# A two-layer language tower on one core: sums in the output tensor, norm weights in the products, halved second-tile products, identity products between two passes

## The chip, the cores and the metric

The kernel runs on one core of a Trainium2 chip. The metric is the device time of one execution in microseconds (us). The core has a matmul engine (TensorE, PE in the rows; PEld is its weight load), a vector engine (VectorE, DVE), an activation engine (ScalarE, ACT), a general engine (GpSimd, POOL) and an engine that only issues transfers (SyncE, SP). Each runs its own instruction stream in order; they meet at semaphores. Matmuls write into eight PSUM banks; DVE and ACT read them; POOL cannot.

## What is computed

A batch of 32 sequences of 128 tokens, 192 features each, goes through an embedding and four blocks, each with a residual sum. Cut to what matters here:

```
h = layernorm(emb[x] * sqrt(192) + positions)
h = h + quantised_attention(layernorm(h))       # 12 heads of 16; softmax(scores) is rounded to 8 bits with one
                                                # scale for the whole tensor, so it needs two passes over the scores
h = h + three_expert_attention(layernorm(h))
h = h + latent_block(layernorm(h)):
    lat = silu(rmsnorm(x, ln_w) @ w_comp);  q, k, v = lat @ w_qkv
    out = linear attention of elu(q)+1, elu(k)+1, gated v, with a decay per head    # scores * decay, then times v
    x = x + (rmsnorm(out, memn_w) @ w_proj) * silu(lat @ w_outgate)
    x + (silu(rmsnorm(x, ffn_ln_w) @ w1) * (rmsnorm(x, ffn_ln_w) @ w2)) @ w3
h = h + attention(...) and then a mixture of 8 experts, 2 per token:
    out = x + sum over its 2 experts of weight * (gelu(xm @ w1[e] + b1[e]) @ w2[e] + b2[e])
```

`rmsnorm(x, w)` multiplies the normed features by a vector `w` before the product, so `w` may as well stand in the rows of the weight matrix.

## The kernel before

The stages run one after the other. The embedding and the quantised attention work on eight groups of four 128-token tiles. **The second pass of the quantised attention** (`tensor_attn`, from the function `turn_terms` on) follows the first when all row sums are known: DVE forms the largest reciprocal of a sum, PE turns it across the partitions in `tensor_tops(pe, SUM_TOP, 0, 1)` (L315, L317), DVE makes three bf16 terms of each row's exponent offset (L463 to L467), PE turns these (L625, `turn_terms`), ACT takes them (L726), and then, for each of 32 tiles, PE forms scores in four banks (L640, L641: products of 32 rows), ACT takes exponentials of 128x384 (L735), DVE adds a shift (L481), and PE multiplies by the values (L650, L654).

**The latent block** works on 16 pairs of tiles. Two streams, each with its own four banks and buffers, take turns: while one runs the first part of a pair (`tensor_l_1`, `scalar_l_1`, `vector_l_1`, `pool_l_1`), the other runs the second part (`..._l_2`), and `alternate` writes their pieces into each engine's one stream in turn at every `yield`. Of the first part matter here: normed rows are turned (`turn`, L966), ACT takes them out of PSUM multiplied by `l_lnw` (`take_turned`, L977, one instruction for each half of the features), PE forms the latent (L1007) and from it q, k, v and the gates (L1718, L1721). Later `products` (L1662) makes 12 score matrices of a tile: for each of three `k`, four products of 32 rows, one for each bank `j`. `decayed` (L1577) multiplies each bank of 384 columns by the decay and writes it to SBUF. This is done for tile 0 and then for tile 1 in the same four banks: the second `products` waits until DVE has read all four banks, and the second `decayed` waits until all 12 products are there. Between the two `products` stands half of the other stream's last product (L1759), and behind the second the other half. Then `times_v` (L1672) multiplies both tiles by the values, waiting first for all eight `decayed` steps; ACT takes the result (L1819), PE turns it back (L1680), DVE divides (L1586 to L1588), and PE turns it once more.

Of the second part matter: `turn_doubled` (L985, L987) turns the normed rows of the feed-forward, `take_doubled` (L993) takes them out of PSUM multiplied by `l_fnw`, again one ACT instruction for each half, and `hidden` (L1690 with 128 rows, L1698 with 64 rows) multiplies by w1 and w2. The tables of this block are made by `vector_l_tables` on DVE, behind the last but one piece of the three-expert stage; its last step folds `memn_w` into `w_proj` (L1425).

**The expert stage** sorts the tokens' rows by expert into a DRAM tensor, `moe_rows_in`, and takes 39 groups of 256 rows, the last of each expert filled up with unused rows of weight 0. Meanwhile the residual rows have been written to another DRAM tensor, `moe_sum` (in the code `acc`; L2020, a POOL transfer for each pair). For each group PE runs L2359, L2364, two turns (L2346, L2347) and L2374; DVE weights the results (L2262) into one of three buffers `x_y`; POOL issues two indirect transfers that add 128 rows each to `moe_sum` (L2291) and waits for them to land before the next group. Unused rows are sent to spare rows behind row 4095. DVE may refill a buffer when the adds of three groups earlier have landed. SP loads the next group's weights. At the end SP waits for all adds, copies `moe_sum` to the output (L2332) and waits for that copy.

The wait that splits the two tiles of the latent block, and the end of the program:

```
if i >= 1:
    pe.wait_ge(f.decayed, per(g, 4 * M, 4 * i))        # products, tile 1
v.wait_ge(f.qk_p, per(g, M, i + 1))                    # decayed
pe.wait_ge(f.decayed, per(g, 4 * M, 4 * M))            # times_v, both tiles
...
sp.wait_ge(x_add, 32 * NX)
sp.dma_start(flat(out...), flat(acc[0:T * P, :])).then_inc(x_end_st, 16)
sp.wait_ge(x_end_st, 16)
```

Of the kernel before, what the change touches and what calls it, by code (L numbers as in the profile page):

```python
# [6 lines left out]
F32 = mybir.dt.float32  # L7
# [88 lines left out]
def tower(nc, a, out):  # L96

    with ExitStack() as ctx:
# [437 lines left out]
        def tensor_attn(pe):  # L536
# [80 lines left out]
            tensor_tops(pe, SUM_TOP, 0, 1)  # L617

# [371 lines left out]
        def take_doubled(a, b, dst, ready, scale):  # L990

            for c in range(2):
                ins = nc.scalar.activation(dst[:, c, :], a.bank[b][:, c * NM:(c + 1) * NM], ACT.Identity, scale=scale[:, c:c + 1])  # L993
            ins.then_inc(ready, 1)
# [413 lines left out]
        def vector_l_tables(v, ch):  # L1408

            yield  # L1410
            v.wait_ge(s_wf, 16 * len(loads_f + loads_l))
            ch.step(nc.vector.tensor_scalar(l_qkn, l_qkn, ROOT_SCALE, None, ALU.mult))
            for s in range(2):
                w = l_qkn[:, s * DH:(s + 1) * DH]
                nc.vector.tensor_tensor(l_cw[:, s, :], l_rot[:, 0:DH], w, ALU.mult)
                nc.vector.tensor_tensor(l_sw[:, s, 0:8], l_rot[:, 16:24], w[:, 8:16], ALU.mult)
                nc.vector.tensor_tensor(l_sw[:, s, 8:16], l_rot[:, 24:32], w[:, 0:8], ALU.mult)
            v.wait_ge(l_s1, 1)
            ch.step(nc.vector.tensor_scalar(l_ld, l_ld, 1.0, None, ALU.add))
            ch.step(nc.vector.reciprocal(l_ld, l_ld))  # L1420
            ch.step(nc.vector.tensor_scalar(l_ld, l_ld, 0.65, 0.3, ALU.mult, ALU.add))
            ch.step(nc.vector.tensor_scalar(l_ld, l_ld, 1e-5, 0.999, ALU.max, ALU.min))
            nc.vector.tensor_scalar(l_dt, l_ld, -1.0, 1.0, ALU.mult, ALU.add).then_inc(l_s0, 1)
            for c in range(2):
                ins = nc.vector.tensor_scalar(lw_proj[0:C, c, :], lw_proj[0:C, c, :], l_memn[0:C, c:c + 1], None, ALU.mult)  # L1425
            ch.step(ins)
# [146 lines left out]
        def decayed(v, g, a, f, i):  # L1573

            v.wait_ge(f.qk_p, per(g, M, i + 1))
            for j in range(4):
                nc.vector.tensor_tensor(a.p[:, 4 * i + j, :], a.bank[j][:, 0:384], decay[:, j, :],  # L1577
# [75 lines left out]
        def products(pe, g, a, f, i):  # L1653
# [3 lines left out]
            if i >= 1:  # L1657
                pe.wait_ge(f.decayed, per(g, 4 * M, 4 * i))
            for k in range(3):
                for j in range(4):  # L1660
                    s = slice(32 * j, 32 * j + 32)
                    mm = nc.tensor.matmul(a.bank[j][:, k * P:(k + 1) * P], a.ts[s, i, 3 + k, :], a.ts[s, i, k, :],  # L1662
                                          start=True, stop=True)
            mm.then_inc(f.qk_p, 1)

        def times_v(pe, g, a, f, i):

            pe.wait_ge(f.value, per(g, 1, 1))
            pe.wait_ge(f.decayed, per(g, 4 * M, 4 * M))
# [112 lines left out]
        def scalar_l_1(act, g, a, f):  # L1782
            act.wait_ge(f.xT_p, per(g, 3, 1))
            take_turned(a, 0, a.xT, f.xT, scale=l_lnw)
# [43 lines left out]
        def scalar_l_2(act, g, a, f):  # L1828
# [4 lines left out]
            take_doubled(a, 2, a.xT, f.xT, l_fnw)  # L1833
# [176 lines left out]
        def send(pool, g, a, f):  # L2010
# [9 lines left out]
            pool.dma_start(acc[bass.ds(pair * (M * P), M * P), :].rearrange("(t p) d -> p t d", p=P),  # L2020
# [171 lines left out]
        acc = nc.dram_tensor("moe_sum", (T * P + NR, D), F32).ap()  # L2192
# [94 lines left out]
        def pool_x(pool):  # L2287
            for k in range(NX):
                pool.wait_ge(x_out, k + 2)
                for t in range(NT):  # L2290
                    pool.indirect_dma_start(out=acc, out_offset=bass.IndirectOffsetOnAxis(  # L2291
                        ap=x_id[k % B3][:, t:t + 1].bitcast(U32), axis=0), in_=x_y[k % B3][:, t, :], in_offset=None,
                        compute_op=ALU.add).then_inc(x_add, 16)
                pool.wait_ge(x_add, 32 * (k + 1))

        def sync_x(sp):
# [34 lines left out]
            flat = lambda x: x.rearrange("r d -> (r d)").rearrange("(p n) -> p n", p=P)  # L2331
            sp.dma_start(flat(out.rearrange("t p d -> (t p) d")), flat(acc[0:T * P, :])).then_inc(x_end_st, 16)  # L2332
            sp.wait_ge(x_end_st, 16)
# [223 lines left out]
```

## Time and profile before

| | |
|---|---|
| median of 3 runs | 1969.83 us (1968.5 to 1972.9) |
| profiled execution, its own time | 1969.73 us |
| its span, first to last instruction | 1968.1 us |
| mean granted clock of TensorE | 0.892 of full |
| busy share of the span: PE / DVE / ACT / POOL | 79% / 66% / 49% / 24% |
| second pass of the quantised attention | about 352 to 424 us |
| latent block | about 684 to 1178 us, a period of 56.9 us for two pairs |
| expert stage, groups | about 1610 to 1950 us |
| copy to the output | from 1955.8 us to the end |

```text
span 1968.1 us, 37567 instructions
## 1 busy us (share of the span) xinstructions
PE 1551.7 (79%) x13020; PEld 1205.5 (61%) x13020; DVE 1289.9 (66%) x4233; ACT 961.6 (49%) x2769; POOL 481.7 (24%) x689
## 2 busy tenths in 40 slices
PE   0076764888888758888888877999999949999996
PEld 0032221776666546666666656777777738888885
DVE  7898885787888767877877744666666642222221
ACT  1275999873545445554454423444444414444442
POOL 7401333000000012222222211222222223333332
PEclk9985555559999869999999988999999969999998
DMA  3000000119991000000000000000000038778785
GB/s 74 18 1 1 1 1 1 22 42 172 183 174 11 0 1 1 0 0 0 0 0 0 0 10 18 26 25 24 24 24 24 25 89 199 190 193 199 189 197 137
DMA packets 136263, 113.02 MB, mean 57 GB/s; under 512 B 29416, under 2 KB 128456, under 8 KB 136136
## 3 DMA queue, kind: packets, MB, share of 16 engines
q1 hardware_dynamic: 119320, 91.70, 20.3%
q0 software_dynamic: 16864, 20.33, 5.4%
q8 instruction: 42, 0.69, 0.1%
q14 instruction: 37, 0.30, 0.1%
HBM read 69.19 MB, written 45.94 MB: 59 GB/s over the span
## 4 chain that ended last, share of the span: by engine, by line
PE 46%; DVE 34%; ACT 12%; issue 4%; POOL 2%; DVEq 0%; DMA 0%; ACTq 0%; POOLq 0%; SPq 0%
ACT bank L716 9%; PE bank L2374 8%; PE bank L2364 6%; PE bank L1007 5%; PE bank L2359 3%; PE bank L1000 3%; PE bank L2030 2%; PE bank L1690 2%; DVE R L1577 2%; DVE WK L1577 2%; DVE R L1882 2%; PE bank L966 1%; PE bank L640 1%; PE bank L641 1%; PE bank L1718 1%
## 5 line engine op out<-in xcount | busy, mean ns | idle before, releaser
L1047 POOL TENSOR_TENSOR WK<-WK,mhalf 128x2 f32<-128x2 f32 (+1 forms) x96 | 78.7, 819 | 546.0 <-DVE WK L1024 247.1
L2411 ACT ACTIVATE R<-bank,R 128x256 f32<-128x256 f32 x234 | 98.5, 472 | 187.1 <-PE bank L2364 185.5
L716 ACT ACTIVATE bank<-bank,nbias,sc 128x128 f32<-128x128 f32 x384 | 168.9, 952 | 21.6 <-POOL nbias L528 21.6
L2291 POOL DMA_INDIRECT moe_sum<-WK x78 | 121.5, 1558 | 229.0 <-DMA moe_sum<-WK 166.2
L2262 DVE SCALAR_TENSOR_TENSOR WK<-bank,R,WK 128x192 f32<-128x192 f32 x78 | 28.9, 412 | 207.6 <-PE bank L2374 207.6
L716 ACT ACTIVATION_READ_ACCUMULATOR bank<-bank,nbias,sc 128x1 f32 x384 | 162.1, 726 | 0.0
L2374 PE MATMUL bank<-R 128*128 128x192 f32 x936 | 158.6, 326 | 0.0
L1007 PE MATMUL bank<-WK,R 96*128 96x256 f32 x576 | 147.5, 398 | 6.2 <-ACT WK L973 3.5
L2374 PEld LDWEIGHTS bank<-R 128*128 128x128 f32 x936 | 151.3, 190 | 0.1
L1007 PEld LDWEIGHTS bank<-WK,R 96*128 96x128 f32 x576 | 106.2, 194 | 25.9 <-ACT WK L973 6.6
L2364 PE MATMUL bank<-R 128*128 128x256 f32 x468 | 113.0, 392 | 0.0
L610 PE MATMUL bank<-R 32*128 32x128 bf16 x384 | 62.8, 300 | 60.1 <-ACT bank L716 57.2
L610 PEld LDWEIGHTS bank<-R 32*128 32x128 bf16 x384 | 29.5, 118 | 118.7 <-ACT bank L716 106.6
L2364 PEld LDWEIGHTS bank<-R 128*128 128x128 f32 x468 | 86.8, 192 | 23.8 <-issue 13.2
L433 DVE TENSOR_REDUCE neg_all<-bank 128x3 f32<-128x384 f32 x128 | 69.4, 554 | 27.4 <-PE bank L610 25.2
L528 POOL TENSOR_SCALAR nbias<-neg_all,sc 128x3 f32<-128x3 f32 x128 | 38.8, 303 | 197.6 <-DVE neg_all L433 197.3
L559 PE MATMUL bank<-R,wq 96*128 96x512 bf16 x192 | 79.4, 542 | 4.6 <-DVE WK L407 2.7
L1000 PE MATMUL bank<-R,WK 96*128 96x192 f32 x384 | 76.4, 343 | 2.9 <-ACT WK L973 1.4
L1690 PE MATMUL bank<-WK,R 128*128 128x256 f32 x256 | 65.5, 400 | 15.0 <-ACT WK L993 15.0
L315 PE MATMUL bank<-ident,amx 128*1 128x128 f32 (+2 forms) x5 | 1.9, 382 | 93.6 <-DVE amx L351 54.8
L2140 ACT ACTIVATE WK<-bank,R 128x256 f32<-128x256 f32 x96 | 40.3, 471 | 69.4 <-PE bank L1007 69.4
L966 PE MATMUL bank<-ident,WK 128*96 128x128 f32 x320 | 53.0, 290 | 26.1 <-DVE WK L1899 11.6
(507 smaller groups left out, 4131.3 us busy)
## 6 DMA issues: line engine op xcount, KB each, us to landing
moe_rows_in<-zeros SPq DMA_DIRECT2D x1, 25026.0 KB, 147.2
R<-in_L_ffn_w SPq DMA_DIRECT2D x39, 576.0 KB, 5.0
R<-in_L_ffn_w SPq DMA_DIRECT2D x39, 384.0 KB, 3.1
R<-moe_rows_in SPq DMA_DIRECT2D x39, 194.0 KB, 4.6
R<-in_L_ffn_w SPq DMA_DIRECT2D x78, 96.0 KB, 3.7
R<-in_L_ffn_b SPq DMA_DIRECT2D x39, 96.0 KB, 5.1
moe_sum<-resid POOLq DMA_DIRECT2D x16, 192.0 KB
moe_sum<-WK POOLq DMA_INDIRECT x78, 5.9
```

The lines of the kernel that those rows point to most:

```text
L559: mm = nc.tensor.matmul(bank[b][:, :], wq[0:C, c, o * P:(o + 1) * P], tokens(xqT_all, g)[0:C, c, :], start=(c == 0), stop=(c == 1))
L610: mm = nc.tensor.matmul(bank[u % 4][:, k * P:(k + 1) * P], qk[32 * j:32 * j + 32, k, i * P:(i + 1) * P], qk[32 * j:32 * j + 32, 3 + k, i * ...
L716: ins = nc.scalar.activation(s, s, ACT.Exp, bias=nbias[:, u, k:k + 1], scale=col(SS), accum_out=units(sum_all, g, u)[:, k:k + 1])
L1000: mm = nc.tensor.matmul(a.bank[b][:, i * D:(i + 1) * D], a.xT[0:C, c, i * P:(i + 1) * P], w[0:C, c, :], start=(c == 0), stop=(c == 1))
L1007: mm = nc.tensor.matmul(out, w[0:C, c, m], a.xT[0:C, c, :], start=(c == 0), stop=(c == 1))
L1047: nc.gpsimd.tensor_tensor(a.rs[:, 0:n], a.ve[:, 0:n], mhalf[:, 0:n], ALU.pow).then_inc(f.root, 1)
L1577: nc.vector.tensor_tensor(a.p[:, 4 * i + j, :], a.bank[j][:, 0:384], decay[:, j, :], ALU.mult).then_inc(f.decayed, 1)
L1690: mm = nc.tensor.matmul(a.bank[c][:, out], w[:, c * P:(c + 1) * P], a.xT[:, 0, :], start=(p == 0 and w is lw_1a), stop=(p == 1), skip_grou ...
L2291: pool.indirect_dma_start(out=acc, out_offset=bass.IndirectOffsetOnAxis(ap=x_id[k % B3][:, t:t + 1].bitcast(U32), axis=0), in_=x_y[k % B3] ...
L2364: mm = nc.tensor.matmul(hidden_at(p, n), xw_1a[h][:, q * P:(q + 1) * P], x_T[h][:, 0, :], start=False, stop=True)
L2374: mm = nc.tensor.matmul(bank[7][:, t * D:(t + 1) * D], x_hid[f][:, t * P:(t + 1) * P], xw_2[h][:, f, :], start=(p == 0 and n == 0 and t == ...
L2411: ins = nc.scalar.activation(x_hid[q], hidden_at(p, n), ACT.Gelu, bias=xb_1[h][:, q:q + 1])
```

## The change

Four things change.

- **The output itself takes the sums.** `moe_sum` is gone. The residual rows are written to the output, the indirect adds go to the output, and the copy at the end with its wait is gone. The output has no spare rows, so the adds carry a bound: an index behind row 4095 is dropped.
- **Norm weights are folded.** `vector_l_tables` multiplies the rows of `lw_comp` by `l_lnw` and those of w1 and w2 by `l_fnw` (six more DVE instructions); `take_turned` of the latent stage and `take_doubled` become one plain copy of both halves each.
- **The second tile's products come in two halves**: banks 0 and 1 as soon as DVE has read these two, then banks 2 and 3, each with its own signal; `decayed` of tile 1 waits for the half that it reads. `times_v` of tile 0 waits for five `decayed` steps instead of eight (it writes bank 0, which the fifth reads).
- **Sixteen identity products** of 128x128 float32 into bank 6, which nothing reads, stand on PE between `tensor_tops(pe, SUM_TOP, 0, 1)` and `turn_terms(0)`.

```
             tensor_tops(pe, SUM_TOP, 0, 1)
+            for _ in range(16):
+                nc.tensor.matmul(bank[6][:, 0:P], ident[:, :], ident[:, :], start=True, stop=True)

-        def take_doubled(a, b, dst, ready, scale):
-            for c in range(2):
-                ins = nc.scalar.activation(dst[:, c, :], a.bank[b][:, c * NM:(c + 1) * NM], ACT.Identity, scale=scale[:, c:c + 1])
-            ins.then_inc(ready, 1)
+        def take_doubled(a, b, dst, ready):
+            nc.scalar.activation(dst, chunks2(a.bank[b][:, :]), ACT.Copy).then_inc(ready, 1)

             nc.vector.tensor_scalar(l_dt, l_ld, -1.0, 1.0, ALU.mult, ALU.add).then_inc(l_s0, 1)
+            for c in range(2):
+                nc.vector.tensor_scalar(lw_comp[0:C, c, :], lw_comp[0:C, c, :], l_lnw[0:C, c:c + 1], None, ALU.mult)
+            for w, c in ((lw_1a, 0), (lw_2a, 0), (lw_1b, 1), (lw_2b, 1)):
+                nc.vector.tensor_scalar(w, w, l_fnw[:, c:c + 1], None, ALU.mult)

         def decayed(v, g, a, f, i):
-            v.wait_ge(f.qk_p, per(g, M, i + 1))
             for j in range(4):
+                if j == 0 or (i and j == 2):
+                    v.wait_ge(f.qk_p, per(g, 3, i + 1 + j // 2))
                 nc.vector.tensor_tensor(a.p[:, 4 * i + j, :], a.bank[j][:, 0:384], decay[:, j, :],

             pe.wait_ge(f.slots_v, per(g, M, M))
-            if i >= 1:
-                pe.wait_ge(f.decayed, per(g, 4 * M, 4 * i))
-            for k in range(3):
-                for j in range(4):
...
+            for js in (((0, 1, 2, 3),), ((0, 1), (2, 3)))[i]:
+                if i >= 1:
+                    pe.wait_ge(f.decayed, per(g, 4 * M, js[-1] + 1))
+                for k in range(3):
+                    for j in js:
...
+                mm.then_inc(f.qk_p, 1)

         def times_v(pe, g, a, f, i):
-            pe.wait_ge(f.decayed, per(g, 4 * M, 4 * M))
+            pe.wait_ge(f.decayed, per(g, 4 * M, (5, 8)[i]))

-            take_turned(a, 0, a.xT, f.xT, scale=l_lnw)
+            take_turned(a, 0, a.xT, f.xT)
-            take_doubled(a, 2, a.xT, f.xT, l_fnw)
+            take_doubled(a, 2, a.xT, f.xT)

-            pool.dma_start(acc[bass.ds(pair * (M * P), M * P), :].rearrange("(t p) d -> p t d", p=P),
+            pool.dma_start(sums[bass.ds(pair * (M * P), M * P), :].rearrange("(t p) d -> p t d", p=P),
-        acc = nc.dram_tensor("moe_sum", (T * P + NR, D), F32).ap()
+        sums = out.rearrange("t p d -> (t p) d")
-                    pool.indirect_dma_start(out=acc, out_offset=bass.IndirectOffsetOnAxis(
+                    pool.indirect_dma_start(out=sums, out_offset=bass.IndirectOffsetOnAxis(
                         ap=x_id[k % B3][:, t:t + 1].bitcast(U32), axis=0), in_=x_y[k % B3][:, t, :], in_offset=None,
-                        compute_op=ALU.add).then_inc(x_add, 16)
+                        bounds_check=T * P - 1, oob_is_err=False, compute_op=ALU.add).then_inc(x_add, 16)

             sp.wait_ge(x_add, 32 * NX)
-            flat = lambda x: x.rearrange("r d -> (r d)").rearrange("(p n) -> p n", p=P)
-            sp.dma_start(flat(out.rearrange("t p d -> (t p) d")), flat(acc[0:T * P, :])).then_inc(x_end_st, 16)
-            sp.wait_ge(x_end_st, 16)
```

Line numbers of the kernel after are a few higher: L1662 becomes L1668, L1672 L1678, L1759 L1765.

On PE, in the latent loop, where one stream's second-tile products stand between the two halves of the other's last product; `pair1_21` is the count of `decayed` steps of this stream, `pair1_16` its gated values. Before:

```order
1604 L1759 MATMUL bank<-R,WK 128x192 [waits pair0_30]
1605 L1759 MATMUL bank<-R,WK 128x192 x3
1606 L1658 ISA [waits pair1_33,pair1_19]
1607 L1662 MATMUL bank<-R 128x128 [waits pair1_21]
1608 L1662 MATMUL bank<-R 128x128 x11
1609 L1759 MATMUL bank<-R,WK 128x192 x4
1610 L1669 REGISTER_ALU [waits pair1_16]
1611 L1672 MATMUL bank<-R 32x128 [waits pair1_21]
1612 L1672 MATMUL bank<-R 32x128 x11
1613 L1672 MATMUL bank<-R 32x128 [waits pair1_21,pair1_16]
1614 L1672 MATMUL bank<-R 32x128 x11
```

And in the kernel after:

```order
1607 L1765 MATMUL bank<-R,WK 128x192 [waits pair0_30]
1608 L1765 MATMUL bank<-R,WK 128x192 x3
1609 L1664 ISA [waits pair1_33,pair1_19]
1610 L1668 MATMUL bank<-R 128x128 [waits pair1_21]
1611 L1668 MATMUL bank<-R 128x128 x5
1612 L1664 REGISTER_ALU
1613 L1668 MATMUL bank<-R 128x128 [waits pair1_21]
1614 L1668 MATMUL bank<-R 128x128 x5
1615 L1765 MATMUL bank<-R,WK 128x192 x4
1617 L1678 MATMUL bank<-R 32x128 [waits pair1_21]
1618 L1678 MATMUL bank<-R 32x128 x11
1620 L1678 MATMUL bank<-R 32x128 [waits pair1_21]
```

The twelve second-tile products became two sixes, each behind its own wait for DVE; what stands around them kept its place. On SP, the last rows of the program (`x_add` counts the adds that have landed, `x_end_st` the copy). Before:

```order
168 L2313 DMA R<-moe_rows_in 128x2x194
169 L2325 REGISTER_ALU
170 L2325 COMPARE_AND_BRANCH
171 L2332 DMA out<-moe_sum 48x16384 [waits x_add]
172 L98 UNCONDITIONAL_BRANCH [waits x_end_st]
```

And in the kernel after:

```order
167 L2318 ISA x2
168 L2319 DMA R<-moe_rows_in 128x2x194
169 L2331 REGISTER_ALU
170 L2331 COMPARE_AND_BRANCH
171 L98 UNCONDITIONAL_BRANCH [waits x_add]
```

The copy left the queue, and the end waits for the adds.

## Rows read from the trace of the kernel before

**Rows 1.** Chain of work that ended last, expert stage: start us, us, what

```profile
1923.50 1.50 PE bank L2359 x12
...
1932.12 1.50 PE bank L2359 x12
```

**Rows 2.** Timeline, all engines, the program's end: start us, us, engine, line, operation

```profile
1955.79 0.63 SPq L2332 DMA_DIRECT2D out<-moe_sum  x1
```

**Rows 3.** Waits of the SP queue: line, for what, us in total, times, longest

```profile
SPq L98 <- DMA out<-moe_sum: 11.2, 1, 11.2
```

**Rows 4.** Indirect transfers on POOL, two lines: issue ns min/median/max

```profile
L2291 POOL DMA_INDIRECT moe_sum<-WK x78: 1547/1554/1632, 1622.8 to 1952.3; - x78
...
L2016 POOL DMA_INDIRECT moe_rows_in<-R x64: 956/962/1134, 1242.6 to 1601.6; - x64
```

**Rows 5.** Timeline of POOL, two neighbouring groups of the expert stage

```profile
1667.30 1.55 POOL L2291 DMA_INDIRECT moe_sum<-WK  x1 [5.93 <-issue]
...
1674.99 1.55 POOL L2291 DMA_INDIRECT moe_sum<-WK  x1 [4.28 <-DMA moe_sum<-WK]
```

**Rows 6.** Timeline, all engines, latent block, the first stream's decays

```profile
889.28 1.95 DVE L1577 TENSOR_TENSOR WK<-bank,decay 128x384 f32<-128x384 f32 x4
889.33 1.58 PE L1759 MATMUL bank<-R 128*128 128x192 f32 x8
...
891.29 0.95 PE L1662 MATMUL bank<-R 32*128 32x128 f32 x24 [0.38 <-DVE WK L1577]
892.17 1.58 PE L1759 MATMUL bank<-R 128*128 128x192 f32 x8
892.31 1.95 DVE L1577 TENSOR_TENSOR WK<-bank,decay 128x384 f32<-128x384 f32 x4 [1.07 <-PE bank L1662]
...
894.31 1.52 PE L1672 MATMUL bank<-WK,R 128*32 128x128 f32 x48 [0.56 <-DVE WK L1577]
...
907.83 0.84 ACT L993 ACTIVATE WK<-bank,R 128x256 f32<-128x256 f32 x2 [2.69 <-PE bank L987]
```

**Rows 7.** Chain of work that ended last, latent block, the second stream's turn

```profile
933.86 1.11 PE bank L1213 x10
...
936.50 0.48 ACT WK L993
...
937.02 1.99 PE bank L1690 x8
939.02 1.93 PE bank L1698 x16
```

**Rows 8.** Groups by line and shape, one period of the latent block: busy us, mean ns

```profile
L1662 PE MATMUL bank<-R 32*128 32x128 f32 x96 | 3.8, 287 | 2.8 <-ACT R L1812 2.0 <-DVE R L1577 0.4 <-DVE WK L1577 0.4
...
L973 ACT ACTIVATE WK<-bank 96x512 f32<-96x512 f32 x2 | 1.2, 594 | 0.5 <-PE bank L966 0.5
...
L1559 DVE TENSOR_SCALAR WK<-WK 128x384 f32<-128x384 f32 x2 | 0.7, 360 | 0.1
```

**Rows 9.** Timeline, end of the three-expert stage, DVE's table work

```profile
679.17 0.54 DVE L1425 TENSOR_SCALAR R<-R 96x192 f32<-96x192 f32 x2
...
681.74 0.36 DVE L1199 TENSOR_TENSOR WK<-bank,R 128x192 f32<-128x192 f32 x1 [2.03 <-PE bank L1272]
```

**Rows 10.** Timeline, between the two passes of the quantised attention

```profile
351.47 0.61 PE L625 MATMUL bank<-identb,WK 128*128 128x128 bf16 x4 [5.19 <-DVE WK L467]
```

**Rows 11.** Stretches: us, busy PE, PEld, DVE, ACT, POOL (instructions), PEclk, DMA share, GB/s

```profile
360.00:370.00 10.00, 10.00 (x174) 9.08 (x172) 8.54 (x28) 9.40 (x21) 0.00 (x0) 0.50 0.01 3
...
435.00:436.00 1.00, 1.00 (x14) 0.79 (x12) 1.00 (x3) 0.60 (x1) 0.00 (x0) 0.94 1.05 283
```

**Rows 12.** Chain of work that ended last, second pass (two turns, four tiles apart)

```profile
374.68 0.54 PE bank L625 x4
...
383.57 0.54 PE bank L625 x4
```

**Rows 13.** Chain of work that ended last, latent block's start, at the lower clock

```profile
696.96 0.85 PE bank L1213 x4
```

More of the change, by code:

```diff
@@ L1656, in products @@
             pe.wait_ge(f.slots_v, per(g, M, M))
-            if i >= 1:
-                pe.wait_ge(f.decayed, per(g, 4 * M, 4 * i))
-            for k in range(3):
-                for j in range(4):
[L1661 to L1664, printed above, removed]
+            for js in (((0, 1, 2, 3),), ((0, 1), (2, 3)))[i]:
[3 more added lines that the diff above has]
+                    for j in js:
+                        s = slice(32 * j, 32 * j + 32)
+                        mm = nc.tensor.matmul(a.bank[j][:, k * P:(k + 1) * P], a.ts[s, i, 3 + k, :], a.ts[s, i, k, :],
+                                              start=True, stop=True)
+                mm.then_inc(f.qk_p, 1)
         def times_v(pe, g, a, f, i):
             pe.wait_ge(f.value, per(g, 1, 1))
-            pe.wait_ge(f.decayed, per(g, 4 * M, 4 * M))
+            pe.wait_ge(f.decayed, per(g, 4 * M, (5, 8)[i]))
             for k in range(3):
```

## The prediction, made before the result was known

> **What bounds the kernel now.** The page's chain is spread over all stages, so I read each edited place by itself: first the chain of waits at the end of the program, then the timelines around each edit, and for each asked which wait ends last there.
>
> In the expert stage the chain is PE alone: one group's first product starts 8.62 us before the next group's (1932.12 - 1923.50, [rows 1]), and PE never waits. At the end nothing overlaps: SP sees all adds landed, issues the copy at 1955.79 [rows 2], and then waits 11.2 us for it [rows 3]. In the latent block the chain changes engines all the time; at the decays it goes DVE, PE, DVE, PE [rows 6]. In the second attention pass PE is busy all the time at a granted 0.50, that is 1.2 GHz, and ACT nearly so [rows 11].
>
> **The copy at the end.** Issue 0.63 us and wait 11.2 us go [rows 2, 3]: -11.8 us, all of it on the path. What is late next is the landing of the last add, which was waited for before too. The residual rows are written by the same 16 transfers, only elsewhere, under other work; that costs nothing.
>
> **The bound on the adds.** No transfer with a bound is in the trace. Below zero is possible, since dropped rows are not moved, but I take no gain: PE sets the pace, not these transfers. For the upper end: an indirect transfer of 128 rows takes 0.96 us to issue without an add and 1.55 with one [rows 4]; let the bound cost as much again as the add, 0.59 us. Normally this is hidden: POOL issues two transfers, waits for landing and starts the next group's; where it was late it did so again after 7.69 us (1674.99 - 1667.30, [rows 5]), against PE's 8.62, so it has 0.93 us of slack for each group, or 0.46 for each transfer. The last group has no cover and pays two bounds. I take 0.15 us each, nearer to zero than to 0.59 because no further row data has to be described, as the add does: +0.3. At 0.59, POOL falls behind by 1.18 - 0.93 = 0.25 us a group, 38 groups, +9.5, plus 1.2 at the end: about +11.
>
> **The second tile's products in halves.** In the period of 56.9 us there are two such places, and all 16 pairs have one. As it is: DVE finishes tile 0 at 891.24, PE starts tile 1's products at 891.29, DVE waits 1.07 us and starts at 892.31, ends at 894.26, and only then PE starts `times_v` at 894.31 [rows 6]. All of this is on the chain. After: PE comes out of the other stream's half product (L1759, 889.33 and 1.58) at 890.9, and two banks are read by 890.3, so the first half starts at 890.9 without a wait.
>
> How long is a half? 24 recorded instructions take 0.95 us from first start to last end [rows 6]. One such instruction with all rows of the array takes 0.111 us (1.11 / 10, L1213, [rows 7]), so 24 alone would take 2.7 us: the four banks' products, each on 32 rows of its own, run beside each other. A half uses two of the four row groups. The nearest row for that is `hidden`: L1690 with 128 rows takes 1.99 / 8 = 0.249 us and L1698, two halves of 64 rows in turn, 1.93 / 16 = 0.121 [rows 7]; two run beside each other at full gain. So I take 0.111 / 2 = 0.056 us an instruction: a half occupies PE for 12 x 0.056 = 0.67 us, and since the last one takes 0.287 from its start to its end [rows 8], the half is there after 0.9. Then DVE starts bank 0 at 891.8 instead of 892.31, the second half is there by about 892.5, when DVE has taken two banks, and DVE ends at 893.8: 0.5 us earlier. PE gets to the second L1759 piece at 892.24 (before 892.17), leaves it at 893.8, and finds five decays done: `times_v` starts at 893.8 instead of 894.31, 0.5 us earlier. Bounds: 0.85 if a half is simply half as long (0.48 us) and DVE starts at 891.45; 0.35 if a half takes as long as the whole. I take 0.5.
>
> The Trainium skill, page "TensorE: Matmul & The Clock Gate", Part 3 (packing small matmuls), says that products on distinct row groups run concurrently and gives 3.07 times for four; the same passage speaks against this edit, since a half has only two groups. Worked out as an estimate from half that gain, 1.53, a half would take 12 x 0.111 / 1.53 = 0.87 us on PE and the edit would save about 0.35 instead of 0.5, 5 to 6 us in all instead of 8. The trace's 64-row pairs show the better figure.
>
> Of 16 places, 15 at 0.5 give -7.5. The first pair runs at the lower clock, where PE's share of the gap is larger (a pair of identity products 0.85 / 2 us, [rows 13], against 0.22): I take twice to four times the gain there, -1.5. Nothing is queued behind the new waits on PE but the L1759 half and `times_v`, counted above; on DVE the last residual sum follows, which now waits for L1759 until 893.85, still 0.4 earlier.
>
> **Norm weights.** `take_doubled` is two instructions of 0.84 us together [rows 6], with PE waiting behind them; a plain copy of 96x512 takes 0.594 [rows 8], and I take 0.60 for 128x512: -0.24 each. On the chain it stands in the second stream's turn [rows 7], 8 of 16: -1.9; in the first stream's turn the chain goes through DVE. `take_turned` saves the same, but PE meanwhile works on the other stream's products: 0, except in the first pair, -0.2. The six new DVE steps: two of 96x128, two of 128x512, two of 128x256; from 0.36 us for 128x384 and 0.27 for 96x192 [rows 8, 9] they are about 0.23, 0.45 and 0.29, together 1.9 us. They come before the last 0.54 us step, which ends at 679.71, and then DVE waits 2.03 us, until 681.74 [rows 9]. The cover is just enough: 0; without it, at most +1.9.
>
> **Identity products.** 32 instructions. PE is free from 346.3 until it is wanted at 351.47 [rows 10]. At the full clock 32 x 0.111 = 3.6 us, free of charge. At the lower clock 32 x 0.2125 (0.85 / 4, [rows 13]) = 6.8 us, until 353.1: +1.6, since everything up to the first exponential is one chain. If the clock rises on the way the delay is some 0.3 to 0.8, and turning and the first tiles are faster by about as much. The clock of the pass is the question. PE was busy for 10.00 of 10 us there and stayed at 0.50, while in the next stage it rose, 0.94 in one microsecond [rows 11]; so these products of 32 rows don't raise it, and I take it that they don't hold it either. Net +0.3.
>
> The page named above, Part 1, says that the slow clock is the default and sustained activity releases it. The trace of this pass disagrees for this kind of activity: busy all the time, still 0.50. By the page the identity products would help, and the pass would then stay fast: the second rival.
>
> **Sum**: -11.8 + 0.3 - 7.5 - 1.5 - 1.9 - 0.2 + 0.3 = -22.3. The profiled execution took 1969.73 us, the median is 1969.83; the two agree, so the forecast is 1947.4.
>
> **Rivals.**
>
> The halves give nothing on the chain: L1759 and PE's own occupation (+0.3 us a place) decide, or the other stream's turn is late next. For it: PE is busy for most of the block. Against: DVE's 1.07 us gap is on the chain [rows 6]. The latent block then gives only the folded weights, some -2 to -3: 1955. Chance 0.13.
>
> The second pass holds the full clock. PE then needs about half; ACT, busy 9.40 of 10 [rows 11], becomes the bound. Four tiles take 8.89 us (383.57 - 374.68, [rows 12]), ACT's share 8.36, and there are eight such: -4.2, so 1943. For it: the products stand right ahead of the pass. Against: [rows 11], and PE has a gap behind the products. Chance 0.13.
>
> The bound makes POOL the pace of the expert stage. At 0.59 us for each transfer it takes back 11: 1958, chance 0.06. On the other side: from 0.93 + 23 / 38 = 1.53 us a group, 0.77 for each transfer, it eats the whole gain; at 1.0 it costs 38 x (2.0 - 0.93) + 2 = 43 instead of 0.3, so 1990, slower. For it: the slack of 0.46 for each transfer is small, and dropped rows may need extra work. Against: the whole add costs only 0.59. Chance 0.04.
>
> **How the numbers follow.** The forecast, 1947.4, has 0.64; its own bounds are 1941 (0.85 at every place) to 1951. The others have 0.13, 0.13, 0.06 and 0.04. A range from 1940 to 1956 takes in the first three cases and leaves out about 0.15. A measurement of this kernel can tell some 0.2%, 3.9 us, from no change. Only the last case is slower: 0.04; between it and 1958 some 0.02 lie within 0.2%; faster 0.94.
>
> **What would show it.** In the profile after: the last event is the landing of the last add, and no transfer to the output stands behind it. L2291 should show 1.6 to 1.8 us; above 2.0, and POOL starts that drift behind DVE's results, would prove the bound costly. DVE's 1.07 us wait for products should shrink to about 0.5, `times_v` should start with no wait right behind L1759, and the period should be 55.7 instead of 56.9 us. The pass should show 0.50 again, and four tiles 8.9 us. I am wrong if the period doesn't shrink, if the pass shows 1.00, or if L2291 sets the pace of the groups.

## The result, and the profile after

The changed kernel takes 1960.9 us (median; 1958.3 to 1963.8), the kernel before 1972.6 in the same comparison: a ratio of 0.9946, 95% interval 0.9933 to 0.9959. It is faster, but by about half of what was forecast: 1947.4, with a range from 1940 to 1956, which the result lies above. In the two profiled executions the span went from 1968.1 to 1961.2 us, by 6.9 us, where the sum said 22.3. (The profiled execution of the kernel before is one of its shorter ones and that of the changed kernel one of its longer ones, so the medians, 11.7 us apart, differ by more than the traces do.) The missing 15 us are sought in these two traces, at the places that the prediction named.

**The end.** The last transfer in the timeline of POOL, and then the program's closing instructions (line 98: how often, shortest, median, longest ns, first and last start in us), kernel before:

```profile
1952.33 1.55 POOL L2291 DMA_INDIRECT moe_sum<-WK  x1 [0.30 <-issue]
```

```profile
L98 POOLq DRAIN  x1: 4195/4195/4195, 1956.0 to 1956.0; - x1
L98 SPq COMPARE_BRANCH  x1: 38/38/38, 1967.6 to 1967.6; - x1
L98 SPq EVENT_SEMAPHORE  x1: 17/17/17, 1968.0 to 1968.0; - x1
```

The same of the changed kernel:

```profile
1953.91 1.55 POOL L2297 DMA_INDIRECT out<-WK  x1 [0.30 <-issue]
```

```profile
L98 SPq COMPARE_BRANCH  x1: 38/38/38, 1956.6 to 1956.6; - x1
L98 POOLq DRAIN  x1: 4195/4195/4195, 1956.8 to 1956.8; - x1
L98 SPq DRAIN  x1: 13/13/13, 1956.8 to 1956.8; - x1
L98 SPq EVENT_SEMAPHORE  x1: 17/17/17, 1961.2 to 1961.2; - x1
```

SP is free at 1956.6, as forecast; then everything waits for POOL, whose closing drain takes 4.195 us. Before, the same drain of the same length lay wholly under the copy [rows 2, 3]. From the start of the last transfer to the end it was 15.8 us and is 7.3: 8.5 us gained, not 11.5.

**The adds.** The group of the bounded transfers on the page (busy us, mean ns):

```profile
L2297 POOL DMA_INDIRECT out<-WK x78 | 121.5, 1558 | 228.9 <-DMA out<-WK 151.2
```

78 transfers at 1558 ns, against a median of 1554 [rows 4]: the bound costs nothing that can be seen.

**The latent block.** The timeline of the changed kernel, where [rows 6] showed it before:

```profile
888.07 1.95 DVE L1582 TENSOR_TENSOR WK<-bank,decay 128x384 f32<-128x384 f32 x4
888.11 1.58 PE L1765 MATMUL bank<-R 128*128 128x192 f32 x8
889.62 1.38 PE L1668 MATMUL bank<-R 32*128 32x128 f32 x24
890.61 1.95 DVE L1582 TENSOR_TENSOR WK<-bank,decay 128x384 f32<-128x384 f32 x4 [0.59 <-PE bank L1668]
890.93 1.58 PE L1765 MATMUL bank<-R 128*128 128x192 f32 x8
892.44 1.52 PE L1678 MATMUL bank<-WK,R 128*32 128x128 f32 x48
893.88 0.62 DVE L1513 BATCH_NORM_STATS2 WK<-resid 128x6 f32 x2 [0.65 <-DVE amx L1050]
```

DVE waits 0.59 us instead of 1.07, PE starts the halves and `times_v` (L1678) with no wait. Here the edit does what was forecast. Yet the block as a whole became longer: from the first pair's turning to the last it took 427.56 us before (726.59 to 1154.15) and 430.75 after (725.35 to 1156.10). These are stretches of the changed kernel (us, busy PE, PEld, DVE, ACT, POOL, then the granted clock), and the first of the kernel before:

```profile
800.00:900.00 100.00, 87.21 (x774) 68.19 (x775) 76.33 (x225) 45.74 (x126) 26.90 (x52) 0.95 0.00 0
897.00:898.00 1.00, 1.00 (x8) 0.72 (x5) 0.34 (x2) 0.76 (x4) 0.58 (x1) 0.61 0.00 0
898.00:900.00 2.00, 2.00 (x8) 1.98 (x7) 0.00 (x0) 0.66 (x2) 0.12 (x1) 0.50 0.00 0
901.00:902.00 1.00, 1.00 (x8) 0.90 (x6) 0.96 (x3) 0.24 (x1) 0.00 (x0) 1.00 0.00 0
```

```profile
800.00:900.00 100.00, 83.29 (x786) 63.74 (x785) 78.07 (x229) 49.48 (x137) 26.33 (x52) 1.00 0.00 0
```

Before, the clock was 1.00 throughout. Now it falls to 0.50, that is 1.2 GHz, near 839, 897, 955, 1013 and 1071 us, once in each period from there on, for 6.8 or 3.4 us in turn. What did PE do just before? Its timeline at the turning (L968; the time in brackets is the gap ahead) of the second stream (782.01, 837.88, 896.70) and of the first stream (the others), and below it the second stream's turning in the kernel before. No fall follows the first two rows; one follows 837.88 and one 896.70:

```profile
782.01 0.64 PE L968 MATMUL bank<-ident,R 128*96 128x128 f32 x4 [1.61 <-DVE R L1593]
809.65 0.64 PE L968 MATMUL bank<-ident,R 128*96 128x128 f32 x4 [0.99 <-DVE R L1593]
837.88 0.64 PE L968 MATMUL bank<-ident,R 128*96 128x128 f32 x4 [1.59 <-DVE R L1593]
868.48 0.64 PE L968 MATMUL bank<-ident,R 128*96 128x128 f32 x4 [0.99 <-DVE R L1593]
896.70 0.64 PE L968 MATMUL bank<-ident,R 128*96 128x128 f32 x4 [1.58 <-DVE R L1593]
925.67 0.64 PE L968 MATMUL bank<-ident,R 128*96 128x128 f32 x4 [0.99 <-DVE R L1593]
```

```profile
898.32 0.64 PE L966 MATMUL bank<-ident,R 128*96 128x128 f32 x4 [1.33 <-DVE R L1588]
```

Counted from the start of the first tile's decays, PE now starts `times_v` 0.66 us earlier (892.44 - 888.07 against 894.31 - 889.28), but the turning only 0.41 us earlier (896.70 - 888.07 against 898.32 - 889.28). DVE has the next pair's statistics (L1513) in its queue ahead of the division that the turning waits for. So the gap grew from 1.33 to 1.58 us, and each of the five falls comes right behind such a gap, though the gap of 1.61 ahead of 782.01 brought none. A fall is dear: the stretch from the turning at 837.88 to the next takes 30.60 us and the one from 896.70 takes 28.97, where the same stretch without a fall (782.01 to 809.65) takes 27.64. Three long falls at 2.96 and two short ones at 1.33 make 11.5 us. The period, counted between the second stream's turnings, is 58.8 us with a long fall (837.88 to 896.70); the prediction named a period that doesn't shrink from 56.9 us as a sign of being wrong.

**The pass.** Chain, then stretches of the changed kernel:

```profile
346.28 6.08 PE bank L619 x32
374.78 0.54 PE bank L627 x4
383.67 0.54 PE bank L627 x4
```

```profile
346.00:352.00 6.00, 5.98 (x32) 5.97 (x33) 4.25 (x10) 0.52 (x1) 0.00 (x0) 0.58 0.44 109
352.00:358.00 6.00, 4.22 (x80) 3.42 (x80) 2.19 (x7) 5.35 (x10) 0.00 (x0) 0.99 0.47 29
360.00:420.00 60.00, 60.00 (x1027) 53.83 (x1027) 51.89 (x164) 56.01 (x116) 0.00 (x0) 0.50 0.02 4
```

The identity products do raise the clock, to 0.99 for 6 us (0.50 there before), and the pass then falls back to 0.50 with PE busy all the time; four tiles take 8.89 us, as in [rows 12]. The first turning ends 0.5 us later than before; the later ones come only 0.1 us late (374.78 against 374.68 [rows 12]).

The 6.9 us in parts, by landmarks of the two traces: +1.65 up to the first turning of the latent block (692.87 before, 694.52 after), -2.9 in the first pair, +3.2 in the rest of the block, -0.4 between there and the last transfer, -8.5 at the end.

### The profile page after: what moved, and what is told of

Its sections match the earlier page's. It is cut to its first block, busy times and chain, and to the rows that moved or that the text cites. A ratio compares the mean times of both kernels' runs of the same rounds, so it can differ in the third digit from the quotient of the medians.

```text
span 1961.2 us, 37710 instructions
## 1 busy us (share of the span) xinstructions
PE 1572.4 (80%) x13052; PEld 1225.5 (62%) x13052; DVE 1289.6 (66%) x4239; ACT 952.7 (49%) x2737; POOL 483.4 (25%) x689
## 4 chain that ended last, share of the span: by engine, by line
PE 42%; DVE 37%; ACT 14%; issue 5%; POOL 2%; DVEq 0%; DMA 0%; ACTq 0%; POOLq 0%; SPq 0%
ACT bank L718 9%; PE bank L2377 8%; PE bank L2367 6%; PE bank L1007 5%; PE bank L1000 3%; PE bank L2362 3%; PE bank L2036 2%; DVE R L1888 2%; PE bank L1765 1%; PE bank L968 1%; PE bank L642 1%; PE bank L643 1%; DVE WK L1030 1%; DVE WK L1888 1%; ACT L1845 1%
## 5 line engine op out<-in xcount | busy, mean ns | idle before, releaser
L2297 POOL DMA_INDIRECT out<-WK x78 | 121.5, 1558 | 228.9 <-DMA out<-WK 151.2
L1000 PE MATMUL bank<-R,WK 96*128 96x192 f32 x384 | 81.4, 359 | 2.7 <-ACT WK L975 1.4
L975 ACT ACTIVATE WK<-bank 96x512 f32<-96x512 f32 x64 | 37.7, 591 | 81.6 <-PE bank L968 81.6
L968 PE MATMUL bank<-ident,WK 128*96 128x128 f32 x320 | 53.9, 294 | 27.0 <-DVE WK L1905 11.6
L1000 PEld LDWEIGHTS bank<-R,WK 96*128 96x128 f32 x384 | 69.3, 207 | 9.5 <-ACT WK L975 6.7
```

Of the source, the lines that this page charges most:

```text
L968: mm = nc.tensor.transpose(a.bank[b][0:C, c * NM + i * P:c * NM + (i + 1) * P], src[:, i, c * C:(c + 1) * C], ident[:, :])
L1000: mm = nc.tensor.matmul(a.bank[b][:, i * D:(i + 1) * D], a.xT[0:C, c, i * P:(i + 1) * P], w[0:C, c, :], start=(c == 0), stop=(c == 1))
L2297: pool.indirect_dma_start(out=sums, out_offset=bass.IndirectOffsetOnAxis(ap=x_id[k % B3][:, t:t + 1].bitcast(U32), axis=0), in_=x_y[k % B3 ...
```

## The experiments

Two theories stand against each other on the falls: the longer gap ahead of the turning brings them, or PE's higher load (87.21 of 100 us against 83.29) or the halves as such do. The rest of the sum is tested part by part. All times are medians beside runs of the kernel before on the same chip.

**The second tile's products in one piece again**, all else as changed.

```diff
-            for js in (((0, 1, 2, 3),), ((0, 1), (2, 3)))[i]:
+            for js in ((0, 1, 2, 3),):
                 if i >= 1:
-                    pe.wait_ge(f.decayed, per(g, 4 * M, js[-1] + 1))
+                    pe.wait_ge(f.decayed, per(g, 4 * M, 4 * i))
```

(and `decayed` and `times_v` wait as before.)

> The changed kernel with the second tile's products in one piece again, as before; the rest of the change stays. In the changed kernel PE's gap ahead of the second stream's turn in the latent loop is 1.58 us (1.33 before) and the granted clock falls to 0.50 once in each period from 839 us on. Theory (the longer gap makes the clock fall): the gap is 1.33 again, the clock stays at 1.00 from 740 to 1150 us, the period is 56.9 - 0.24 = 56.7 us, and the time is 2 to 4 us below that of the changed kernel: the halves' gain of about 8 us goes, and falls of some 10.6 us go with it. Rival (the falls have nothing to do with the halves): the falls stay, and the time is about 8 us above that of the changed kernel.

Measured: 1963.2 us, ratio 0.9962 (0.9948 to 0.9975). The gap is 1.33 us again, and of the five falls one is left, near 1071 us. The time is no better than with the halves, where 2 to 4 us less was expected: in the changed kernel their gain and the falls nearly cancel. The period is 56.9 to 57.0 us, not 56.7, so the folded weights gave nothing here (below).

**The gap filled** with five identity products.

```diff
             turned_back(pe, g, a, f, 1)
+            for _ in range(5):
+                nc.tensor.matmul(a.bank[1][:, 0:P], ident[:, :], ident[:, :], start=True, stop=True)
             pe.wait_ge(f.out, per(g, M, M))
```

> The changed kernel with five identity products of 128x128 float32 (1.1 us at the full clock) on PE in the latent block, behind the second tile's turning back and ahead of the wait for DVE: they fill most of the 1.58 us gap and nobody waits for them. Theory (the gap makes the clock fall): the clock stays at 1.00 from 740 to 1150 us, each period is about 55.9 us, as the first one of the changed kernel was that had no fall, and the time is 10 to 11 us below that of the changed kernel: 1950 us. Rival (PE's higher load makes it fall, 87 us busy of 100 against 83): the load rises further, to some 91, the falls stay or become more, and the time is the changed kernel's or above.

> The changed kernel with the gap filled by five identity products, once more, so that the next three stand beside it on one chip: 22 to 24 us below the kernel before, no fall of the clock between 740 and 1150 us.

Measured: 1949.5 us, ratio 0.9891 (0.9865 to 0.9918), and 1950.3, 0.9883 (0.9866 to 0.9899), when run once more beside the last three. A stretch, and the gap in the timeline:

```profile
800.00:900.00 100.00, 90.67 (x829) 71.37 (x830) 79.23 (x233) 47.99 (x135) 27.30 (x53) 1.00 0.00 0
```

```profile
894.30 0.64 PE L968 MATMUL bank<-ident,R 128*96 128x128 f32 x4 [0.47 <-DVE R L1593]
```

PE is busier than ever, 90.67 of 100 us, and the clock stays at 1.00 from 740 to 1150 us: the load is not the cause. The block's main part takes 419.57 us (725.79 to 1145.36), 11.2 less than in the changed kernel. That is the largest missing piece, and its size is that of the five falls.

**One product in the gap instead of five**; else the same edit.

> The changed kernel with one identity product in the gap instead of five: the gap in the second stream's turn is about 1.36 us instead of 1.58, nearly that of the kernel before, and PE's load stays that of the changed kernel. Theory (the length of the gap decides): none or one fall of the clock between 740 and 1150 us, as with the halves undone, and the time is 1949 to 1953 us. Rival (the falls come from what the halves do to PE's work around the gap): five falls, as in the changed kernel, and 1961 us.

Measured: 1953.2 us, ratio 0.9896 (0.9878 to 0.9914), with one fall. PE's gap in its timeline, and the stretch of the fall:

```profile
891.98 0.64 PE L968 MATMUL bank<-ident,R 128*96 128x128 f32 x4 [1.37 <-DVE R L1593]
```

```profile
949.00:954.00 5.00, 4.87 (x19) 4.15 (x18) 1.86 (x4) 1.37 (x6) 0.36 (x1) 0.66 0.00 0
```

A single product of 0.22 us, which shortens the gap nearly to what it was before, takes four of the five falls away. (This trace is of the shortest of four executions, 1950.5 us; the longest took 1956.0 us and may have had more falls.) The halves' work around the gap is unchanged, so they are not the cause by themselves.

**The gap stretched in the kernel before.**

```diff
                 ch.step(nc.vector.tensor_scalar(den, ps[:, :, DH], 1e-5, None, ALU.max))
+                if i == 1:
+                    ch.step(nc.vector.tensor_scalar(den, den, 1e-5, None, ALU.max))
```

> The kernel before with one more DVE step of 128x12 on the chain in each turn of the latent block (the bound on the second tile's denominators is applied twice): PE's gap ahead of the turning grows by about 0.25 us, from 1.33 to 1.58 in the second stream's turn, as in the changed kernel, and nothing else is changed. Theory (the gap makes the clock fall): granted clocks of 0.50 appear behind that gap in most periods, at 1.1 to 2.8 us each, so the time is 4 us for the steps and some 10 for the falls above the kernel before: 1982 to 1986. Rival (PE's load, or the halves as such): no falls, only the 16 x 0.25 us: 1976 to 1977.

Measured: 1988.6 us, ratio 1.0081 (1.0056 to 1.0107). The gaps are 1.54 and, in the other stream's turn, 1.20 us, and there are seven falls between 740 and 1150 us. A gap in the timeline, and the stretch of the first fall:

```profile
907.18 0.64 PE L966 MATMUL bank<-ident,R 128*96 128x128 f32 x4 [1.54 <-DVE R L1590]
```

```profile
788.00:791.00 3.00, 3.00 (x14) 2.68 (x14) 0.48 (x3) 1.79 (x6) 0.70 (x1) 0.58 0.00 0
```

Sixteen steps that lengthen the gap by 0.21 us each, 3.4 us together, cost 16. No part of the change is in this kernel: a longer gap at the turning is enough to bring falls. Two of the seven come behind gaps of 1.20, so the length of one gap is not all that counts.

**The gap filled in the kernel before** (the five products, no other edit).

> The kernel before with the five identity products in the gap ahead of the turning, as in the run with the gap filled. The kernel before shows no fall of the clock in the latent loop (gap 1.33 us). Theory (the products are worth something only where the clock falls): the period stays 56.9 us and the time is within 2 us of the kernel before. Rival (the products help in another way, by keeping the clock up elsewhere or PE warm for what follows): the time is 8 us or more below the kernel before.

Measured: 1971.3 us beside 1974.4, ratio 0.9977 (0.9966 to 0.9988). The period stays 56.95 us, no fall. The 3 us are more than the theory gave. The runs of the kernel before beside it spread from 1972.0 to 1980.3, with the products from 1967.2 to 1973.5, so the kernel before may lose something to falls in some executions; its only trace shows none, and this stays open.

**The end of the copy alone**, in the kernel before: the output takes the sums, the adds have the bound, the copy is gone; the lines are those of the change.

> The kernel before with the sums built in the output, the bound on the adds and no copy at the end, and nothing else of the change. By the prediction: 11.5 us below the kernel before. By the drain of 4.2 us that the copy used to hide: from the last transfer's start to the end 7.3 us instead of 15.8, so 8.5 us below it; the adds at 1.55 us each as before.

Measured: 1967.4 us beside 1974.4, ratio 0.9965 (0.9950 to 0.9980): 7.0 us below, and 11.5 lies outside the interval. From the last transfer's start, 1958.54, to the end of the span, 1965.9, it is 7.3 us: the drain's 8.5, not 11.5. The trace also has three short falls in the latent block, behind gaps of 1.33 us (900.46, the first); so 1.33 is at the edge, with none in the kernel before, one with the halves undone, three here.

```profile
902.00:906.00 4.00, 4.00 (x15) 3.74 (x15) 1.31 (x4) 0.61 (x3) 0.00 (x0) 0.57 0.00 0
```

**POOL's last wait removed**, in the hope of starting the drain earlier.

```diff
-                pool.wait_ge(x_add, 32 * (k + 1))
+                if k < NX - 1:
+                    pool.wait_ge(x_add, 32 * (k + 1))
```

> The changed kernel without POOL's own wait for the landing of the last group's adds; the end of the program still waits for them on SP. In the changed kernel SP sees the last add landed at 1956.6 us, POOL's closing drain runs from 1956.8 for 4.2 us, and the span ends at 1961.2; before, the same drain of 4.2 us lay under the copy. Theory (the drain is a fixed 4.2 us behind POOL's last instruction, and it became the end): it starts right behind POOL's last transfer, about 1.1 us earlier, and the span from the last transfer's start to the end shrinks from 7.3 to 6.1 or 6.2 us. Rival (the drain waits for transfers on their way): its end stays where it is, 7.3 us behind.

One run: span 1962.4 us. The last transfer in POOL's timeline, and the closing instructions:

```profile
1956.06 1.55 POOL L2297 DMA_INDIRECT out<-WK  x1 [0.30 <-issue]
```

```profile
L98 POOLq DRAIN  x1: 7712/7712/7712, 1954.5 to 1954.5; - x1
L98 SPq COMPARE_BRANCH  x1: 38/38/38, 1958.8 to 1958.8; - x1
L98 SPq EVENT_SEMAPHORE  x1: 17/17/17, 1962.4 to 1962.4; - x1
```

The span ends 6.3 us behind the last transfer's start instead of 7.3: the rival is out. The drain's record is longer because POOL's queue reaches it while the transfers are still being issued; it ends at 1962.2, 4.6 us after the last transfer's issue (1956.06 + 1.55), where the drain alone is 4.2. So it follows POOL's last work by a nearly fixed time, and the wait that the edit took away is worth 1 us. From a single execution this is a reading of a trace, not a measured gain.

**Without the identity products** (the loop of sixteen removed).

> The changed kernel without the identity products between the two passes. If they do what the trace of the changed kernel shows (the first tiles at the full clock until about 357 us, 0.50 from there on, the first wanted product 0.5 us later), the time is within 0.5 us of the changed kernel's. If they are worth something later, the time is above it by more than 2 us.

Measured: 1963.2 us, ratio 0.9955 (0.9937 to 0.9973), span 1961.2, that of the changed kernel. The median is 2.3 us above that of the changed kernel, but the two intervals overlap, so the products are worth nothing that can be told. The five falls are there in the same places.

**Halves undone and the gap filled**: both edits above.

> The changed kernel with the gap filled and the second tile's products in one piece again: what the halves are worth once the clock holds. By the prediction 0.5 us at each of 16 places and more in the first pair: 8 to 9 us above the run with the gap filled and the halves, with periods of 56.9 us instead of 55.9. If the halves gave nothing on the chain: within 2 us of it.

Measured: 1962.1 us, ratio 0.9948 (0.9931 to 0.9964), 12 us above the run with halves and filled gap. The turning of the same pair in two neighbouring periods, here and with the halves:

```profile
810.66 0.64 PE L968 MATMUL bank<-ident,R 128*96 128x128 f32 x4
867.67 0.64 PE L968 MATMUL bank<-ident,R 128*96 128x128 f32 x4
```

```profile
810.92 0.64 PE L968 MATMUL bank<-ident,R 128*96 128x128 f32 x4
866.89 0.64 PE L968 MATMUL bank<-ident,R 128*96 128x128 f32 x4
```

A period of 57.01 us against 55.97; the main part of the block takes 427.92 against 419.75. The halves are worth 8.2 us there once the clock holds, so the first rival is out. The first pair gives 1.0 us more (31.82 against 30.85); the other 2.6 us between the medians lie elsewhere in these executions and were not placed.

**Norm weights not folded, the gap filled**: `take_doubled` and `take_turned` as before, the six table steps gone.

> The changed kernel with the gap filled and the norm weights not folded: the two scaled copies of each turn are back (0.84 us instead of 0.60) and the six table steps are gone. By the prediction 1.9 to 2.1 us above the run with the gap filled, with 0.24 us for each period. By the trace with the halves undone, where the period stayed at 56.9 us with the folding: DVE's own chain is as long, the copy's gain goes into a wait, and the time is within 0.5 us of the run with the gap filled.

Measured: 1953.2 us, ratio 0.9893 (0.9875 to 0.9911). The intervals overlap, so the time decides nothing; the trace does: 419.79 us for the main part of the block (726.07 to 1145.86) against 419.75. The folding is worth nothing on the chain. The time that it saves stands again as PE's wait ahead of the first tile's products, which wait for ACT; with the folding and the filled gap, and then without the folding:

```profile
801.11 0.95 PE L1668 MATMUL bank<-R 32*128 32x128 f32 x24 [1.27 <-ACT R L1820]
```

```profile
801.53 0.95 PE L1666 MATMUL bank<-R 32*128 32x128 f32 x24 [1.05 <-ACT R L1818]
```

The clock does not fall behind these gaps of 1.27 us.

**The first pair warmed**: the filled gap, and identity products where PE waits at the start of the block.

```diff
+            first = isinstance(g, int) and g == 0 and a.n == 0
+            if first:
+                stirred_f(streams[1], 14)
             pe.wait_ge(f.xr, per(g, 1, 1))
...
+            if first:
+                stirred_f(streams[1], 9)
             pe.wait_ge(f.cat, per(g, M, M))
             pe.wait_ge(f.gates, per(g, 1, 1))
+            if first:
+                stirred_f(streams[1], 9)
```

> The changed kernel with the gap filled, and beside that identity products on PE at the start of the latent block, where it waits at 0.50: 14 before the first turning, 9 before and 9 behind the wait for the first pair's gates. If they raise the clock for the first pair: its products on the chain, 6.6 us from 694.5 to 701.8 and 9.9 us from 711.5 to 724, take 3.7 and 5.5 us, so up to 7.3 us less than the run with the gap filled; 2.9 if the clock falls again in between; nothing if it stays at 0.50. A loss of 1 to 4 us is possible if they end after they are waited for.

Measured: 1947.9 us, ratio 0.9877 (0.9860 to 0.9893): the lowest median of all, and below both kernels; against the run with the filled gap (0.9883) the intervals overlap.

```profile
684.00:700.00 16.00, 12.93 (x75) 10.67 (x76) 13.94 (x46) 11.63 (x31) 6.80 (x17) 0.90 0.01 2
700.00:712.00 12.00, 5.93 (x49) 5.07 (x48) 8.10 (x20) 2.53 (x6) 2.04 (x7) 0.68 0.00 0
712.00:724.00 12.00, 10.83 (x107) 8.76 (x108) 7.59 (x26) 4.45 (x10) 1.74 (x2) 0.75 0.00 1
```

The clock was 0.50 in the first and third of these stretches with the gap filled alone; counted from the block's first turning, the next one comes 28.7 us later (691.40 to 720.08) instead of 30.8 (695.69 to 726.54). So the warming is worth 2.1 us in this trace, near the 2.9 expected if the clock falls again in between, and not the 7.3. That the first turning itself came 4.3 us earlier was there before any of these products: PE's last work of the stage ahead, too, began 4.3 us earlier.

## Why the prediction was wrong, point by point

- **The step that failed: "Nothing is queued behind the new waits on PE but the L1759 half and `times_v`, counted above".** For the halves I followed PE to `times_v` and stopped there. Behind it PE gains 0.66 us on the way to the turning, but DVE's part of the way gives only 0.41, so part of a wait that was removed at one place stands at the next: the gap ahead of L968 grew from 1.33 to 1.58 us. I took a wait off the chain for harmless, and the sum has no term for the clock of the block, which was 1.00 before and which I took for given without a reason. The falls behind that gap cost 11.2 us (430.75 - 419.57). Shown from three sides: filled, they go; shortened by one product, four of five go; made in the kernel before, they come.
- The halves themselves were right: 8.2 us in the block once the clock holds, forecast 7.5 for 15 places; DVE's wait is 0.59 us, forecast about 0.5; a period without a fall is 55.89 us (753.76 to 809.65), forecast 55.7. The first pair gained 2.9 us, forecast 1.7.
- **The copy**, a mis-sized term: -11.8, measured -8.5 with the bound's +0.3 in it. SP's wait of 11.2 us [rows 3] was taken for the price, but what ends the program is the last of all engines; POOL's drain of 4.2 us was in the trace of the kernel before, under the copy, and I did not look for it.
- **The norm weights**: the copy takes 0.60 us instead of 0.84, as forecast, but the -1.9 is 0. The second stream's chain through PE [rows 7] had a twin that is as long and ends at ACT's copies, where PE's wait ahead of the first tile's products grew from 1.05 to 1.27 us with the folding. With the halves undone the decays start 19.6 us after the turning in either kernel (889.28 - 869.70 and 890.70 - 871.11).
- The bound: +0.3, measured none. The identity products: +0.3, measured 0.1, and the pass fell back to 0.50, so the second rival is out; the third is out by L2297's 1558 ns.
- The time of the costly bound, 1958, is nearest to the result, and that of the first rival, 1955, comes next, both by accident: the bound costs nothing, and the halves give 8.2 us.
- 1.65 us come from the end of the stage ahead, where the clock was 0.50 from 676 to 684 us (0.69 before). The kernel without identity products shows the same (0.82 over 660 to 684 us), and the kernel before with a filled gap 0.84 against 0.86, so it does not belong to those products. Nor does it belong to the rest of the change: the first turning stands at 695.31 us in the kernel before with a filled gap, and at 692.52 and 692.76 in two variants of the changed kernel (one product in the gap; halves undone, gap filled). What decides it in an execution was not tried.

Put right, the sum for the two traces is +1.65 - 2.9 + 3.2 - 0.4 - 8.5, some -6.9. With the gap filled the kernel stands 22 to 24 us below the one before (0.9891 and 0.9883 of it): the forecast's -22.3, though partly by terms that missed in opposite directions.

## What to carry to other kernels

A wait taken out of PE's queue can come back as a longer wait further down, and there its length matters even off the critical path, since the granted clock may fall behind it and make everything after it dearer: read each gap of PE after an edit, and fill the one behind which the clock falls with products that nobody reads, ending before PE is wanted. A term taken from a closing wait is worth no more than the next engine's last instruction allows: read the closing rows of all engines. And before a copy on the chain is credited, measure the second-longest chain to the same place.

## What the runs showed of the hardware that was not expected

- Gaps of PE of 1.2 to 1.6 us were enough for the granted clock to fall to 0.50, for 3.4 to 6.8 us. Falls between 740 and 1150 us, by the gap in the second stream's turn: none at 0.21 and 0.47 us, none, one and three at 1.33, one at 1.37, five at 1.58, seven at 1.54 with 1.20 in the other stream's turn. Gaps of 1.25 to 1.27 us ahead of L1668, two in each period, had no fall behind them with the gap at the turning filled. What decides beside the length of a gap was not settled. The Trainium skill, page "TensorE: Matmul & The Clock Gate", Part 1 (a second failure mode, depth-cycling), describes a kernel whose PE idles briefly between groups of products, so often that the clock goes back and forth; this trace agrees, with gaps of 1.58 us, though not every such gap brings a fall.
- POOL's closing drain takes 4195 ns in every kernel whose POOL waits for its last transfers; SP's takes 13 ns. The Trainium skill, page "VectorE: DVE Perf Modes" (the drain that can't be avoided), gives the drains of a program's preamble and postamble as constant, about 12 ns, on all engines. SP's agrees, POOL's does not, and the measurement decides; whether the drains recorded here at line 98 are of the kind that the page means is not shown.
- A bound on an indirect add of 128 rows costs nothing in its issue: 1558 ns mean with and without it.
